# Golay correction of sign bits inside a transformer block: a check product per chunk with a syndrome carried over, against one product per pair of chunks and a threshold

## What is computed

```
out = x + attn(xn) + ffn(xn)
attn(x): D  = _fractal_dimension(x)
         x1 = ifft(fft(x) * _wave_filter(D, 256)).real       # a circulant product
         bits = sigmoid(x1 @ W_el + b_el) > 0.5              # 24 bits a token
         corrected = _golay_correct(bits)
         return x1 + corrected @ W_le + b_le
_golay_correct(bits):
         syn = (bits @ H.T > 0.5)                            # 12 of them, H = [A.T, I]
         w = syn.sum(-1)
         flip the first w bits that syn names, if 0 < w <= 3
ffn(x):  gelu(x @ w1 + b1) @ w2 + b2                         # 256 -> 1024 -> 256
```

## Time and profile before

| | us |
|---|---|
| median of 3 runs | 413.42 |
| lowest, highest | 413.11, 413.96 |
| the profiled execution, its time | 413.44 |
| its span, first to last instruction | 411.6 |
| TensorE matmul busy | 404.9 (98%) |
| VectorE busy | 308.8 (75%) |
| ScalarE busy | 218.5 (53%) |
| GpSimd busy | 71.9 (17%) |

### The profile page before, as it was taken

The page is one execution under the profiler, slowest core; times in us unless marked ns, Lnnn a source line. Parts: engine busy times, 40 slices in busy tenths (PEclk is TensorE's granted clock), DMA queues, the critical chain, the costliest instruction groups (busy, mean ns, idle before and its releaser), DMA issues.

```text
span 411.6 us, 5546 instructions
## 1 busy us (share of the span) xinstructions
PE 404.9 (98%) x1770; PEld 325.0 (79%) x1785; DVE 308.8 (75%) x505; ACT 218.5 (53%) x325; POOL 71.9 (17%) x100
## 2 busy tenths in 40 slices
PE   7999999999999999999999999999999999999996
PEld 4887788888878888788888878888788887878874
DVE  7889986867768695786968678686776868676654
ACT  3966536555454655536555454655536654464541
POOL 2143301212002121111212012121111212012000
PEclk9999999999999999999999999999999999999999
DMA  7553333213332113232123333023333111111011
GB/s 196 205 192 117 104 102 102 59 45 103 104 102 84 65 56 102 102 102 99 43 63 102 102 102 101 26 77 102 102 102 101 52 52 51 52 52 51 2 51 51
DMA packets 15343, 35.78 MB, mean 87 GB/s; under 512 B 5452, under 2 KB 6628, under 8 KB 15332
## 3 DMA queue, kind: packets, MB, share of 16 engines
q1 hardware_dynamic: 15188, 35.52, 26.9%
q10 hardware_dynamic: 144, 0.13, 0.1%
HBM read 27.19 MB, written 8.45 MB: 87 GB/s over the span
## 4 chain that ended last, share of the span: by engine, by line
PE 91%; DVE 4%; DMA 2%; POOL 1%; issue 1%; ACT 1%; SPq 0%; DVEq 0%
PE p_h L893 41%; PE p_f L911 26%; PE p_f L916 13%; PE p_s L948 5%; PE p_l L937 3%; PE p_s L967 2%; DMA rows_sb<-rows_dram 1%; DMA x_sb<-x 1%; DMA rows_dram<-row_nums 1%; DVE stats L571 1%; POOL row_nums L358 0%; DVE h_lo L613 0%; DVE xn L593 0%; DVE xn L598 0%; DVE xT_lo L603 0%
## 5 line engine op out<-in xcount | busy, mean ns | idle before, releaser
L435 ACT ACTIVATE h<-p_h,small_sb 128x512 f32<-128x512 f32 x128 | 88.2, 689 | 153.4 <-PE p_h L893 152.0
L613 DVE TENSOR_TENSOR h_lo<-h,h_hi 128x512 fp32r<-128x512 f32 x128 | 90.0, 704 | 65.1 <-ACT h_hi L443 65.0
L911 PE MATMUL p_f<-h_hi,w_hi 128*128 128x512 f32 x254 | 99.3, 391 | 0.0
L911 PE MATMUL p_f<-h_hi,w_lo 128*128 128x512 f32 x254 | 98.9, 389 | 0.0
L893 PE MATMUL p_h<-xT_hi,w_hi 128*128 128x512 f32 (+1 forms) x258 | 85.7, 413 | 0.0
L443 ACT CAST h_hi<-h 128x512 fp32r<-128x512 f32 x128 | 79.4, 620 | 5.8
L893 PE MATMUL p_h<-xT_hi,w_lo 128*128 128x512 f32 (+1 forms) x258 | 79.4, 389 | 0.0
L893 PE MATMUL p_h<-xT_lo,w_hi 128*128 128x512 f32 (+1 forms) x258 | 79.2, 388 | 0.0
L916 PE MATMUL p_f<-h_lo,w_hi 128*128 128x512 f32 x254 | 78.2, 389 | 0.0
L366 POOL TENSOR_TENSOR uv<-xn 128x512 f32<-128x512 f32 x30 | 44.5, 1503 | 128.8 <-DVE xn L598 128.8
L893 PEld LDWEIGHTS p_h<-xT_lo,w_hi 128*128 128x128 f32 x258 | 48.3, 188 | 10.5 <-DVE xT_lo L772 0.2
(11 more groups left out here) (115 smaller groups left out, 319.9 us busy)
## 6 DMA issues: line engine op xcount, KB each, us to landing
xt_sb<-xt SPq DMA_DIRECT2D x16, 512.0 KB, 5.3
x_sb<-x SPq DMA_DIRECT2D x15, 512.0 KB, 4.5
rows_sb<-rows_dram SPq DMA_DIRECT2D x15, 512.0 KB, 4.4
out<-xt_sb SPq DMA_DIRECT2D x15, 512.0 KB, 2.9
xt_sb<-w SPq DMA_DIRECT2D x3, 512.0 KB, 7.7
xt_sb<-w SPq DMA_DIRECT2D x2, 256.0 KB, 4.5
x_sb<-x SPq DMA_DIRECT2D x2, 128.0 KB, 2.3
x_sb<-x SPq DMA_DIRECT2D x1, 256.0 KB, 3.0
```

Of the source, the lines that this page charges most:

```text
L435: nc.scalar.activation(h[m % 2][:], p_h[:, m % 2, :], ACT.Gelu, bias=small_sb[:, S_B1 + m:S_B1 + m + 1]).then_inc(gelu_done, 1)
L613: nc.vector.tensor_tensor(h_lo[m % HR][:], h[m % 2][:], h_hi[m % HR][:].bitcast(F32), ALU.subtract).then_inc(h_lo_done, 1)
L911: mm(p_f[:, a, :], w[:, m, a * HF:(a + 1) * HF], h_hi[r][:], start=(m == 0 and w is w2_hi), stop=False, skip_group_check=True)
```

## The change

The correction goes by pairs of chunks. `cw` becomes two matrices: the latents of the even chunk go to partitions 0 to 31 (high) and 64 to 95 (low) of `p_l`, those of the odd chunk are added to the same bank at 32 to 63 and 96 to 127. One `latents_rest`, one `take_bits` (64 partitions), one check product and one `correct` serve both chunks. The check matrix gives one linear form of the bits for each corrected bit, compared with 9.5: for bit i of the first 12 the weights are 512 on itself, -16 on the other first bits, 12 on bit 12 + i and -1 on the other last bits; for bit 12 + i it is 16 on itself. There are no syndromes to carry over, so `take_checks`, the tile row of ones and `checks(16)` are gone. `cor` becomes fp32r with 128 rows, and `W_le` is split in two fp32r parts (`le2`, one tile for each chunk of the pair) in place of three bf16 parts. The matmuls of `le_products` are as many as before. `latent` is laid out four times over the partitions.

```diff
-        cor = sb("cor", [ROWS, CTOK], BF16)
-        le3 = sb("le3", [ROWS, 2, HF], BF16)
+        cor = sb("cor", [P, CTOK], F32R)
+        le2 = [sb(f"le2_{i}", [P, 2, HF], F32R) for i in range(2)]
...
-            def take_bits(c, par):
-                dve.wait_ge(rest_done, c + 1)
-                nc.vector.scalar_tensor_tensor(out=word[SEG * par:SEG * par + LAT, :], in0=p_l[0:LAT, :],
+            def take_bits(p):
+                dve.wait_ge(rest_done, p + 1)
+                nc.vector.scalar_tensor_tensor(out=word[0:PAIR, :], in0=p_l[0:PAIR, :],
...
-            def correct(c, gone=1):
-
-                dve.wait_ge(checked, c + 1 + gone)
-                nc.vector.tensor_scalar(cor[:], p_g[0:ROWS, :].bitcast(U32), TOP_WORD, None,
-                                        ALU.is_gt).then_inc(cor_done, 1)
-
-            def take_checks(c):
-                dve.wait_ge(checked, c + 1)
-                nc.vector.tensor_scalar(word[3 * SEG:3 * SEG + SYN, :], p_g[3 * SEG:3 * SEG + SYN, :], 0.5, None,
-                                        ALU.is_gt).then_inc(syn_done, 1)
+            def correct(p):
+                dve.wait_ge(checked, p + 1)
+                nc.vector.tensor_scalar(cor[:], p_g[:, :], 9.5, None, ALU.is_gt).then_inc(cor_done, 1)
...
-            def latents(c, par, first=False):
-
-                if not first:
-                    pe.wait_ge(bits_done, c)
+            def latents(par, p):
+
+                if par == 0 and not (isinstance(p, int) and p == 0):
+                    pe.wait_ge(bits_done, p)
                 n = 0
                 for xp in (xT_hi, xT_lo):
                     for k in range(KB):
-                        last = mm(p_l[:, :], cw[:, k, :], xp[par][:, k, :], start=(n == 0), stop=(n == 2 * KB - 1))
+                        last = mm(p_l[:, :], cw[par][:, k, :], xp[par][:, k, :], start=(par == 0 and n == 0),
+                                  stop=(par == 1 and n == 2 * KB - 1), skip_group_check=True)
                         n += 1
-                last.then_inc(lat_done, 1)
+                if par == 1:
+                    last.then_inc(lat_done, 1)
...
+            def checks(p):
+
+                pe.wait_ge(bits_done, p + 1)
+                mm(p_g[:, :], code[:], word[:], start=True, stop=True).then_inc(checked, 1)
+
+            def le_products(par, p):
+
+                pe.wait_ge(cor_done, p + 1)
                 for a in range(2):
-                    last = mm(p_s[:, a, :], le3[:, a, :], cor[:], start=False, stop=True, skip_group_check=True)
+                    last = mm(p_s[:, a, :], le2[par][:, a, :], cor[:], start=False, stop=True, skip_group_check=True)
```

More of the change, by code:

```diff
@@ L443, in hidden_hi, with even_chunk, odd_chunk @@
                 nc.scalar.copy(h_hi[m % HR][:], h[m % 2][:]).then_inc(h_hi_done, 1)
-            def chunk(c, par):
+            def even_chunk(c):
+                for m in range(MB):
+                    gelu(c, m)
+                    hidden_hi(c, m)
+                    if m == 1:
+                        turned_hi(c)
+                    if m == 4:
+                        columns_hi(c + 1, 1)
+            def odd_chunk(c, p):
                 for m in range(MB):
@@ L453, in chunk, with first_branch_chunk, last_chunk @@
                     if m == 4:
-                        columns_hi(c + 1, 1 - par)
-            def first_branch_chunk(c, par):
+                        columns_hi(c + 1, 0)
+            def first_branch_chunk(c, p):
+                for m in range(MB):
+                    gelu(c, m)
+                    hidden_hi(c, m)
+                    if m == 1:
+                        latents_rest(p, first=True)
+                    if m == 2:
+                        turned_hi(c)
+                    if m == 4:
+                        columns_hi(c + 1, 0)
+            def last_chunk(c, p):
                 for m in range(MB):
@@ L460, in first_branch_chunk @@
                     if m == 0:
[L461 to L473, removed]
+                        latents_rest(p)
                     if m == 1:
@@ L1142, in constants @@
                   [1, 0, 0, 1, 1, 0, 0, 1, 1, 0, 0, 1], [0, 1, 1, 0, 0, 1, 1, 0, 0, 1, 1, 0]], np.int64)
-    rows = np.concatenate([a.T, np.eye(SYN, dtype=np.int64)], axis=1)
-    codes = np.zeros((P, 2, P), f4)
-    fixed = np.zeros((P, GROUPS, SEG), f4)
-    for par in range(2):
-        here, before = SEG * par, SEG * (1 - par)
-        codes[here:here + LAT, par, ROWS:ROWS + SYN] = rows.T
-        fixed[:] = 0.0
-        fixed[before:before + LAT, :, 0:LAT] = 25.0 * np.eye(LAT)[:, None, :]
-        fixed[2 * SEG, :, 0:LAT] = 9.5
-        fixed[ROWS:ROWS + SYN, :, 0:SYN] = (1.0 - 13.0 * np.eye(SYN))[:, None, :]
-        codes[:, par, 0:ROWS] = fixed.reshape(P, ROWS)
-    return np.eye(P, dtype=f4), con, basis, codes.reshape(P, 2 * P)
+    assert a.sum(axis=1).min() >= 4
+    one = np.zeros((SEG, SEG), f4)
+    for i in range(SYN):
+        one[0:SYN, i] = -16.0
+        one[SYN:LAT, i] = -1.0
+        one[i, i] = 512.0
+        one[SYN + i, i] = 12.0
+        one[SYN + i, SYN + i] = 16.0
+    codes = np.zeros((P, P), f4)
+    for q in range(2):
+        for twice in range(2):
+            at = PAIR * q + SEG * twice
+            codes[SEG * q:SEG * (q + 1), at:at + SEG] = one
+    return np.eye(P, dtype=f4), con, basis, codes
 def layouts(inputs):
```

281 lines of the change are left out of this document (148 added, 133 removed).

## The result

The changed kernel takes 411.05 us in the median (410.08 to 412.22, six runs), the kernel before 413.28 us beside it. The ratio is 0.9945, with a 95% interval of 0.9935 to 0.9955. The profiled execution took 411.11 us, 2.33 us less than that of before, where 3.58 us were forecast. So the kernel is faster, and the time is 0.15 us above the range on record.

The account below looks back on a forecast made before the run. TensorE was taken as the bound. Checks 2.38, LE products 0.27 and the stall of chunk 1 0.93 sum to 3.58 us, taking 413.44 us to 409.86, stated as 409.9 us; range 409.2 to 410.9.

Parts of the forecast that it names:

- Checks: Check products on TensorE: 17 become 8, and the nine that go save 2.38 us, all on the path.
- LE products: The 16 `le_products` pairs in fp32r go from 0.47 to 0.453 us each, a gain of 0.27 us.
- rival 4: Only the bare matmul pace is saved: 2.04 us for checks, nothing from the type switch; 410.5 us, chance 0.10.
- Rival 2: The longer fp32r weight loads of `le_products` show on TensorE, costing 2.9 us: 412.7 us, chance 0.04.
- The stall of chunk 1: TensorE's wait at `latents(1)` for `take_bits(0)` to leave `p_l` disappears, gaining the full 0.93 us.
- Setting up: Before the loop: extra `cw` writes, 43 KB more table loads and added memsets are covered and count 0.
- The cover of `add_ffn(0)`: On VectorE in chunk 1, `add_ffn(0)` ends 0.3 us before `down(1, 0)` needs it, the change's smallest cover.
- rival 1: Chunk 1's stall comes back elsewhere, above all at `add_ffn(0)` or a later `hidden_lo`; 410.3 or 410.8 us, chance 0.20.
- All other covers: Waits in the loop stay covered, 2.87 us at the check and 4.2 us at `correct`; wider partitions cost no more.
- Rival 3: Slower than before: the pair's bits reach the check late in 8 odd chunks, stalling TensorE; 416.3 us, chance 0.02.

Follow-up runs that it names:

- The kernel with the copy first: Changed kernel with ScalarE's copy of the circulant (`c_f`) moved ahead of the high part of chunk 1's columns; 411.19 us, ratio 0.994.
- the kernel with both edits: Changed kernel with the `c_f` copy ahead of the high part of chunk 1's columns and the `W_le` split behind `add_ffn(0)`; 411.06 us, ratio 0.9939.
- the profile with the hold: Changed kernel with x of chunk 2 and later loads held until chunk 1's row-number broadcast has landed; 410.43 us, ratio 0.9928.
- moving the split: Changed kernel with VectorE's two `W_le` split subtractions moved from ahead of chunk 1's statistics to behind `add_ffn(0)`; 410.29 us, ratio 0.9919.
- the small table: Changed kernel with `latent` cut to 24 rows, other partitions zeroed: 410.54 us; with `codes` also back at 128 KB: 410.32 us.
- five times the table: Kernel before with the 128-row latent table loaded five times, the extra tile behind all others; 413.84 us, ratio 1.0004.

## Why the prediction had the direction right and the gain 1.25 us too large

**Checks: right.** 2.40 us measured for 2.38.

**LE products: the term was mis-sized.** "16 pairs thus go from 0.47 to 0.453 us: a gain of 16 x 0.017 = 0.27 us, from the switch of type that disappears" is a loss of 0.10 us, an error of 0.37. The pair takes 0.47 us in either kernel, 0.473 after and 0.466 before. The step took the 0.02 us above the pace for a cost of the switch; the pair keeps it when the switch is gone, so it belongs to something else, which no run here names. That nothing comes from the switch was rival 4's part; its other part, checks at the bare pace of 2.04 us, did not come. Rival 2 is refuted: the loads grew from 98 to 190 ns, and the pairs lost 0.1 to 0.2 us where it had 2.9.

**The stall of chunk 1: the mechanism right, but a step before it failed.** The failing step is in "Setting up", which ends with "I count 0 for these": it let the row numbers of chunk 1 come as before, and they came 1.08 us later. Its one cover, 1.05 us ahead of `latents(0)`, was that of the writes of `cw`. The chain that matters runs through ScalarE: row numbers, centring, `xT_hi`, `c_f`, latent weights. In the kernel before, the copy ends at 29.59 + 0.37 = 29.96 and TensorE uses it at 30.44, so that chain had 0.48 us of cover, and the prediction did not look for it. Centring 1.08 us later used that up and passed on the rest, 0.6 to 0.75 us. Over the profiles with late rows this is a line: `filtered(0)` starts 11.74 us after the centring, at 26.60, 26.90, 26.99, 27.20, 27.53 and 28.07 alike (38.34, 38.64, 38.72, 38.94, 39.27, 39.80). The kernel with the copy first has 11.74 too (26.93, 38.67), but its latent weights do not wait for the copy, so there it says nothing; the kernel with both edits is 0.4 us lower. Where the centring is before about 26.4, `filtered(0)` stays at 38.22 to 38.45 (26.27, 26.19, 26.05, 25.96), as TensorE gets to the latent weights at 30.47 to 30.70 by itself. In the kernel before it is 12.99 us after a centring at 26.12, 26.31 or 26.74. For one at 25.66 or 25.59, where the filter was late, it is at 39.32 and 39.87. So with equal rows the change is worth 0.9 us there on early rows, as forecast, and 1.25 on late ones; the profiles before and after compare early rows with late ones.

**The cover of `add_ffn(0)`: eaten by the same lateness.** "That is 0.3 us early: covered" was a loss of 0.15 us in the profile. L635 starts at 38.84, while TensorE is 0.75 us later; VectorE's queue lost the centring's whole 1.08 us. With early rows the cover is there: in the profile with the hold `add_ffn(0)` ends at 38.97 and is wanted at 39.58, and from `filtered(0)` to `filtered(1)` it takes 23.41 us. With late rows, moving the split gets it back. This is rival 1 as it was named, for 0.15 us; its larger part, 0.75 us, came at a place that it did not name.

**All other covers: right.** No wait for bits or for `cor` in the loop; 64 and 128 partitions cost what 24 and 96 did. The rest on ScalarE takes 596 ns, for 590. On VectorE `take_bits` takes 717 ns for 724, and `correct` 683 for 680. Rival 3 needed 3.4 us more here and found none.

**The size, put together.** The profile with the hold is the forecast's own case: stall of chunk 1 0.89 us, checks 2.40, LE products -0.10, in all 3.19 us, 410.25 us. From the forecast 409.86 that is 0.39 us, of which the LE term is 0.37 and the stall 0.04; the checks gave 0.02 more. The rest, to 411.1, is the lateness of the row numbers: 0.72 us at `filtered(0)` and 0.15 at `add_ffn(0)`. How much of that a job shows differs. The two other jobs of the changed kernel have medians of 410.68 and 410.72 us, inside the range on record, and so has the median of all 18 runs, 410.80; that the first came out above it is in part the draw.

**What stays open.** Why the rows are later in the changed kernel. All eight profiles of it that had the large `latent` and no hold have the centring at 26.60 or later; the two with the small table have 26.05 and 26.27, and of six profiles of the kernel before and its variants without a hold five are at 26.31 or earlier. That looks like a shift and not like one unlucky draw. It goes with the table in the changed kernel, but five times the table made the rows no later in the kernel before, and the intervals of the small-table kernel and of the changed one overlap. Bytes alone are not the cause; whether it is the partitions that the table lands on, or another thing that changed with it, no run separates.

## What to carry to other kernels

When a stall goes, list the cover of every chain that ends at that place, those through DMA first, and ask what late arrival each can take; a cover worked out on one path says nothing of the next. A wait in the DMA queue behind a transfer that the compute waits for may bring it earlier: 4.14 and 4.60 us with the wait, for 4.93 to 6.15 in the changed kernel without it. In the kernel before, 4.40 us lies among the 3.7 to 4.8 of the profiles without it, and in neither kernel is a gain in time clear of the noise. Ask also what an earlier start will run beside: early rows slowed the filter here. Where the gain hangs on a DMA early in the program, one profile is one draw: read two or three before the sum is trusted to a tenth of a microsecond.

## What the runs showed of the hardware

**Place of tiles.** An unused tile of 4,112 bytes a partition, ahead of the others, made each chunk 0.09 us longer (24.85 for 24.77), 1.3 us in all, with the same instructions. TensorE's starts with the tile:

```profile
137.44 0.39 PE L949 MATMUL p_s<-uv_hi,c_hi 128*128 128x512 f32 x1
...
138.84 0.62 PE L894 MATMUL p_h<-xT_hi,w_hi 128*128 128x512 f32 x2
```

The six products take 1.40 us; without the tile they take 1.36 (137.10 to 138.46). With the same tile behind all others a chunk took 24.77 us again. A study that adds a buffer should put it last.

**Small transfers vary.** The 4 KB store of the row numbers of chunk 1 took from 2.14 to 3.24 us until the spread was issued, the spread and what follows up to the centring 3.7 to 6.2 us.

**Some operations of VectorE and GpSimd take longer beside each other.** The filter above is one case: 0.19 us by itself and 1.17 us beside the centring. In the loop it is `uv` on GpSimd; chunk 5 before, then after:

```profile
148.12 2.94 POOL L366 TENSOR_TENSOR uv<-xn 128x512 f32<-128x512 f32 x2 [9.20 <-DVE xn L598]
...
149.88 2.27 DVE L603 TENSOR_TENSOR xT_lo<-xn,xT_hi 128x1024 fp32r<-128x1024 f32 x1
```

```profile
147.21 4.00 POOL L364 TENSOR_TENSOR uv<-xn 128x512 f32<-128x512 f32 x2 [9.12 <-DVE xn L603]
...
148.85 1.22 DVE L608 TENSOR_TENSOR xT_lo<-xn,xT_hi 128x1024 fp32r<-128x1024 f32 x1
149.98 1.77 DVE L618 TENSOR_TENSOR h_lo<-h,h_hi 128x512 fp32r<-128x512 f32 x1
```

Before, `xT_lo` is the long one, and after, one `h_lo` in each chunk. Over the kernel the mean of `xT_lo` fell from 2180 to 1248 ns and that of `h_lo` rose from 704 to 811, 14 us each way, and `uv` went from 1503 to 1997 ns. Shapes and counts are those of before. Not every operation is hit: other VectorE work beside `uv` keeps its time. In the loop TensorE waits for none of them, so it cost nothing there; with the early rows of the kernel before it did. That the overlap is the cause is read from where the long ones stand; no run here removes the GpSimd work.
